# Transformer stage: TensorE's order in the even steps, scores and one rotation product ahead of the turned probabilities

## The reference

```
def attn_layer(x, Wqkv, qs, ksc, Wo):
    q, k, v = split(x @ Wqkv)                   # 16 heads x 64
    q, k = l2norm(q) * qs, l2norm(k) * ksc
    q = q * cos * scale + rotate_half(q) * sin * scale
    k = k * cos / scale + rotate_half(k) * sin / scale
    # each window of 32 queries sees its own 32 keys and the 32 before
    sim = q @ k.T * 8, masked
    out = softmax(sim) @ v
    return out @ Wo
for i in range(6):
    x = attn_layer(shift_tokens(x), ...) + x
    x = ffn_layer(shift_tokens(x), ...) + x     # layer norm, a * gelu(gate), W2
```

## Time and profile before

| | us |
|---|---|
| median of 3 runs | 2478.24 |
| lowest and highest | 2477.98, 2493.84 |
| profiled execution | 2483.95 |
| its span, first to last instruction | 2482.2 |
| transformer's 96 steps, in the span | 556 to 2162 |
| mean granted TensorE clock | 0.958 |
| busy: PE, DVE, ACT, POOL | 2266.1, 1930.9, 1256.9, 1161.2 |

### The profile page before, as it was taken

The page is one execution under the profiler, slowest core; times in us unless marked ns, Lnnn a source line. Parts: engine busy times, 40 slices in busy tenths (PEclk is TensorE's granted clock), DMA queues, the critical chain, the costliest instruction groups (busy, mean ns, idle before and its releaser), DMA issues.

```text
span 2482.2 us, 83657 instructions
## 1 busy us (share of the span) xinstructions
PE 2266.1 (91%) x36350; PEld 1536.8 (62%) x36446; DVE 1930.9 (78%) x4287; ACT 1256.9 (51%) x2304; POOL 1161.2 (47%) x855
## 2 busy tenths in 40 slices
PE   8989897888999999999999999989999999869885
PEld 4557554445667676766766676766667666645564
DVE  5742487789998989898988989898989988646712
ACT  3524153345656565656565556556565656325331
POOL 1037300036666556655656555655666555310064
PEclk7989898999999999999999999999999999879898
DMA  9012100010111211121110211111111111220012
GB/s 300 22 30 41 58 2 1 1 31 19 42 27 37 67 45 26 26 67 37 41 36 22 65 45 32 36 57 30 41 36 32 36 29 32 53 87 2 18 38 76
DMA packets 63736, 106.92 MB, mean 43 GB/s; under 512 B 11700, under 2 KB 48831, under 8 KB 56844
## 3 DMA queue, kind: packets, MB, share of 16 engines
q1 hardware_dynamic: 57626, 93.00, 13.2%
q0 software_dynamic: 4736, 8.29, 1.5%
q10 hardware_dynamic: 1010, 0.29, 0.1%
HBM read 42.55 MB, written 13.24 MB: 22 GB/s over the span
## 4 chain that ended last, share of the span: by engine, by line
PE 62%; DVE 17%; POOL 9%; issue 9%; ACT 2%; DMA 1%; SPq 0%; POOLq 0%; DVEq 0%; ACTq 0%
PE ps L2161 9%; PE ps L2264 6%; PE ps L2243 6%; POOL mem L2929 4%; PE ps L2182 4%; PE ps L2205 4%; PE ps L2170 4%; PE ps L2220 3%; PE ps L2323 3%; PE ps L2309 3%; PE ps L2300 2%; PE ps L1171 2%; POOL mem L2942 2%; PE ps L279 2%; PE ps L1655 2%
## 5 line engine op out<-in xcount | busy, mean ns | idle before, releaser
L2929 POOL TENSOR_TENSOR mem<-mem 128x512 f32<-128x512 f32 x384 | 572.6, 1498 | 568.4 <-DVE mem L2461 564.8
L2161 PE MATMUL ps<-mem 128*128 128x512 f32 x768 | 380.3, 607 | 10.2 <-DVE mem L2461 4.2
L2765 ACT ACTIVATE mem<-ps 128x512 f32<-128x512 f32 x384 | 222.5, 606 | 156.7 <-PE ps L2182 156.0
L2744 ACT ACTIVATE mem<-ps 128x512 f32<-128x512 f32 x384 | 221.0, 598 | 122.9 <-PE ps L2161 84.1
L2456 DVE TENSOR_TENSOR mem<-ps,mem 128x512 f32<-128x512 f32 x384 | 259.1, 675 | 11.8 <-ACT mem L2744 11.6
L2461 DVE TENSOR_TENSOR mem<-ps,mem 128x512 f32<-128x512 f32 x384 | 261.7, 681 | 0.0
L2182 PEld LDWEIGHTS ps<-mem 128*128 128x128 f32 x1536 | 184.6, 142 | 112.2 <-issue 95.7
L2243 PEld LDWEIGHTS ps<-mem 64*64 64x64 f32 x12288 | 195.1, 136 | 80.5 <-issue 77.0
L2468 DVE TENSOR_REDUCE mem<-mem 128x16 f32<-128x1024 f32 x192 | 232.3, 1210 | 0.0
L2942 POOL TENSOR_TENSOR mem<-mem 128x1024 f32<-128x1024 f32 x96 | 182.7, 1904 | 96.9 <-DVE mem L2530 96.9
L2182 PE MATMUL ps<-mem 128*128 128x128 f32 x1536 | 213.8, 276 | 4.1 <-POOL mem L2936 2.8
(11 more groups left out here) (304 smaller groups left out, 4158.6 us busy)
## 6 DMA issues: line engine op xcount, KB each, us to landing
mem<-mem SPq DMA_DIRECT2D x48, 768.0 KB, 5.8
mem<-in_Wqkv SPq DMA_DIRECT2D x6, 1536.0 KB, 6.7
mem<-mem SPq DMA_DIRECT2D x36, 256.0 KB, 3.5
y<-mem SPq DMA_DIRECT2D x8, 512.0 KB, 6.4
mem<-in_W12T SPq DMA_DIRECT2D x8, 512.0 KB, 7.6
mem<-y SPq DMA_DIRECT2D x16, 256.0 KB, 4.9
mem<-in_L3W SPq DMA_DIRECT2D x16, 256.0 KB, 5.3
mem<-in_L2Wo SPq DMA_DIRECT2D x6, 512.0 KB, 6.9
```

What stands on the lines that cost most here:

```text
L2161: e.matmul(self.K.ps[:, o, :], self.columns(u, bb), self.K.l2[l % 2]["Wqkv"][:, 512 * i:512 * i + 512], start=True, stop=True, skip_group_ ...
L2765: e.activation(to, view(self.K.ps[:, self.FEATURE[i], :], "p (c q) -> p c q", c=4), ACT.Copy).then_inc(s("placed"), 1)
L2929: e.tensor_tensor(t1[:, cols], t1[:, cols], self.T2[:, cols], ALU.add).then_inc(s("rotated"), 1)
```

## The change

In even steps TensorE issues the first rotation product for step g+3 and the scores of step g ahead of the turn of the last step's probabilities. In phase 6 the rotation product stays behind the turn, because it needs the turn of x issued between the two halves. All other orders, and all other engines, stay as they are.

```
             if half == 0:
+                if turned and w != 6:
+                    self.pe_rotate(e, g + 3, 0)
+                if this:
+                    self.pe_scores(e, g)
                 if last:
                     self.pe_turn_p(e, g - 1, 0)
                 if this:
                     self.pe_beside(e, hl, w, 0)
                 if last:
                     self.pe_turn_p(e, g - 1, 1)
-                if this:
-                    self.pe_scores(e, g)
+                if turned and w == 6:
+                    self.pe_rotate(e, g + 3, 0)
                 if turned:
-                    self.pe_rotate(e, g + 3, 0)
                     self.pe_rotate(e, g + 3, 1)
                 if last:
                     self.pe_weigh(e, g - 1)
```

## The result

| | before | after |
|---|---|---|
| median of 4 runs, us | 2481.81 | 2544.62 |
| lowest and highest | 2477.98, 2493.84 | 2535.60, 2550.55 |
| profiled execution | 2483.95 | 2550.55 |
| transformer in the span, first to last scores | 556.3 to 2162.1: 1605.7 | 558.9 to 2230.4: 1671.5 |
| mean granted TensorE clock | 0.958 | 0.953 |

The changed kernel takes 1.0247 of the time before (95%: 1.0219 to 1.0274), 63 us more. The forecast was 2523 and its range ended at 2542; the time is just above it. In the trace the transformer grew by 65.8 us and the whole span by 66.6, so nothing outside it matters. In kernels whose order carries a condition on the phase they are 6 higher than before's.

What follows compares the result with a forecast made beforehand. It took TensorE and VectorE, both nearly full, to meet without slack at the scaling of the queries. Phases 4, 6, 2 and 0 added 17.4, 14.9, 3.0 and 9.9, together 45, to 2478.24: 2523 us, range 2496 to 2542.

Steps and rivals of the forecast that it cites:

- What bounds the kernel: TensorE and VectorE both nearly full, meeting at VectorE's scaling of the queries with no slack beyond a 0.4 us hand-over.
- Rival A: Whole transformer: TensorE's order alone decides and VectorE catches up; 11 us faster, 2467 us; chance 0.13.
- Rival B: Part of the lateness absorbed: phases 0 and 2 vanish, phases 4 and 6 shrink to 1.1 us; 2504 us; chance 0.12.
- Phase 4: VectorE's copy and maximum come later, delaying the turn to features; +1.45 us, 12 times, 17.4 us.
- the lower bound: If the hand-over can shrink and the turn to features has 0.3 hidden slack: phases 4 and 6 alone, 25 us, 2504.
- Phase 6: Scores wait 0.8 us for ScalarE's last keys, VectorE's maximum comes later; +1.35 us, 11 times, 14.9 us.
- Phase 2: TensorE's 1.6 us wait is gone, yet VectorE's copy comes later; +0.25 us, 12 times, 3.0 us.
- Phase 0: VectorE's copy comes later and carries this through phase 1; +0.9 us, 11 times, 9.9 us.
- rival C: TensorE's clock dips behind new waits in phases 4 and 6, 1.7 us each, 40 us more: 2562 us; chance 0.09.

Runs made afterwards that it cites:

- e3_turnx_first: The changed kernel with phase 6's turn of x ahead of both turns of the probabilities; 2547.29 us, ratio 1.0255 to the kernel before.
- e2_copy_between: The changed kernel with VectorE's copy of the turned probabilities between the two banks' scores in even steps too; 2535.21 us, ratio 1.0207 to the kernel before.
- e8_clamp_before: The kernel before with VectorE's clamp operand read and written in reverse order; 2517.16 us, ratio 1.0020 to the kernel before.
- e6_only4: The kernel before with the changed order in phase 4 alone; 2529.85 us, ratio 1.0076 to the kernel before.
- e7_only6: The kernel before with the changed order in phase 6 alone; 2531.98 us, ratio 1.0088 to the kernel before.
- e1_late6: The changed kernel with phase 6 kept in the order of before; 2529.88 us, ratio 1.0206 to the kernel before.
- e5_only02: The kernel before with the changed order in phases 0 and 2 alone; 2547.99 us, ratio 1.0138 to the kernel before.
- e10_shift: The changed kernel with 64 more small matmuls (128 instructions) once ahead of the loop; 2567.52 us in one run.

## Why the prediction was right and wrong

**What bounds the kernel** was read rightly: TensorE and VectorE meet at L2506 with no slack, and a late copy makes TensorE late. Of an undisturbed half layer the forecast was 3.95 us more, and 4.04 were measured by the medians, 4.7 by the shortest. That the first is so close is partly luck: phase 6 came out 0.6 too low in the forecast and phase 2 0.5 too high. Rival A, TensorE's order alone, is out: it asked for a gain, and of the pairs only the one with phase 2 became shorter, by 0.2. Rival B, a delay partly absorbed, is out too: it had nothing in phase 0 and 1.1 in phases 4 and 6, and 0.96, 1.36 and 1.93 were measured; only the delay of phase 2 vanished as it says.

**Phase 4**, +1.45 forecast, +1.36 measured. All its signs came: L2541 waits 1.98 for L2223 (about 1.2 was expected), L2516 no longer waits, L2164 waits 0.48 for L2521, L2185 for L2506. The hand-over from L2506 to L2185 shrank from 0.42 to 0.05 (1190.04 to 1190.09), as the lower bound allowed.

**Phase 6**, +1.35 forecast, +1.93 measured. The wait for the placement is 1.02 instead of 0.8, and the wait of L2164 for ScalarE's L2740 (0.92) was not seen: the rotation now stands directly behind the turn of x that it needs, since the change takes away the scores between them, which gave ScalarE its time to copy. e3_turnx_first prices what of it was on the path at 0.27.

**Phase 2**, +0.25 forecast, -0.21 measured without a dip. **Phase 0**, +0.9 forecast, +0.96 measured; e2_copy_between takes this back by moving only VectorE's copy, so the working behind it is right.

**The step that failed** is the sum and what it leaves out. It adds four terms for undisturbed phases to the time before, so it takes the disturbances to stay as they are; it has no term for TensorE's instructions arriving late, and it has a falling clock only as an alternative, rival C, at 0.09, with dips in phases 4 and 6 behind the new waits. And phase 2's working, "1.6 us of wait is gone", takes that wait for idle time and prices nothing that it took up. What the runs showed in its place: about 20 us came on top of the forecast's 45. The traces put about 11 of the 17.6 extra us of half layers 1 to 10 with late instructions (waits on issue of 30.0 us after and 18.1 before, and the dips behind some of them) and about 6.5 with dips behind the wait of phase 1 that the wait of 1.60 before the turn had hidden till then, 38.28 with a dip against 38.17 before, 39.6 against 37.95 after.

The dips that cost do not lie where rival C had them. They follow the wait of phase 1, which was there before (the earlier trace rows shows one, of 2.35 us) and is no longer now (22.5 us in 11, against 24.1). Its 6 dips against 3 before are no effect of the change that the runs show: the number is 5, 2 and 2 in e8_clamp_before, e6_only4 and e7_only6, which keep the old order in phases 0 and 2, and 3, 4, 3 and 3 in e1_late6, e3_turnx_first, e5_only02 and e10_shift, which have the new one. What goes with the order is the price: without a late instruction in them, phases 1 and 2 take 38.00 to 38.73 with such a dip (37.32 to 38.40 with none) in the first three, and 38.99 to 39.63 (37.32 to 37.96) in the other four. The section of the Trainium skill that the prediction cited ("TensorE: Matmul & The Clock Gate", "A second HAM failure mode: psum-queue depth-cycling") speaks of frequent short idles between groups. The trace agrees little: of the new short waits in phases 4 and 6 (0.48, 0.92, 1.02 us), 23 phases in all, 3 had a dip in or behind them, and each of these 3 also held a wait on issue of 0.75 to 1.81. The sign that the prediction gave for rival C, a granted clock under 0.98 in the transformer, did not come: it is 0.98, against 0.99 before.

**What stays open.** Why the new order in phases 0 and 2 brings more than twice as many long waits on issue was not worked out. The split of the 20 us between clock and instruction supply is rough: it rests on one execution of each kernel, and a late instruction sometimes brings a dip itself. e10_shift shows that the place of the long waits goes with the position in the program, but a kernel without them was not made.

## What to carry to other kernels

Before moving work forward on one engine, read in what order its consumer takes the results: here scores that were ready some 1.7 us (phase 4) and 2.2 us (phase 6) before VectorE took them were worth nothing, because the consumer's queue had the later turn first, and each even step but phase 2's paid for the detour. Moving the consumer's order along with it (e2_copy_between) took back 2.3 of the 4.0 us per undisturbed half layer, though only some 10 of 61 us in the whole time, and by the intervals perhaps none. Ask also what a wait that is to be removed takes up: here it had hidden the dips of the clock ahead of it. Then add to the forecast what a slack-free kernel shows already as disturbances (clock dips behind waits, waits on issue): they are terms of the sum, not a rival, and their number changes with any change of order.

## What the runs showed of the hardware

- TensorE's instructions can be late. A burst of 128 small products with their weight loads stops for up to 2.1 us, and goes on 1.25 to 1.62 us after a 16 KB transfer of the instruction queue has ended (all 39 waits of over 1 us before, after and in e10_shift). Up to 37 us per execution are such waits (e3_turnx_first), and 128 instructions more ahead of the loop move them to other steps without changing their sum much (31.0 us in 28 waits in e10_shift, 30.0 in 27 in after).
- In the four runs of after the time goes with the mean granted clock: 0.953, 0.954, 0.956, 0.961 with 2550.55, 2545.88, 2543.36, 2535.60 us. In the four of e1_late6 it doesn't: 0.952, 0.953, 0.955, 0.955 with 2534.25, 2525.50, 2535.80, 2523.92.
- The same dip of TensorE's clock costs next to nothing or 1.65 us, as TensorE has a wait behind it that shrinks (1.60 to 0.33 us before) or not (after).
- A clamp of 128 x 32 numbers on VectorE takes up to ten times as long beside additions and a memset on GpSimd (1.79 us against 0.18), whichever way its elements are walked.
- The kernel before took 2480.76, 2513.02 and 2486.71 us on three chips, 1.3% apart, which is as much as a part of this change.
